# Three load groups, a table of dataless matmuls and new turn strings in a two-layer kernel on one core

## What is computed

```python
mod = (_silu(c) @ wmod).reshape(16, 6, 1, -1)        # per layer: shift, scale and gate, twice
h = _layernorm(x) * (1 + ca) + sa
x = x + ga * attn(h)                                 # ga: sign kept, magnitude at least 0.25
h = _layernorm(x) * (1 + cb) + sb
x = x + gb * ffn(h)
```

## Time and profile before

| | us |
|---|---|
| median of 3 runs | 2970.29 (2969.28 to 2974.66) |
| the profiled execution's own time | 2970.33 |
| its span, first to last instruction | 2968.5 |
| loop of 15 rounds, from 201.9 to 2840.9 | 2639.0 |
| mean granted TensorE clock, share of full | 0.907 |

### The profile page before, as it was taken

One profiled execution on the slowest core, in us unless ns is written; L12 is line 12 of the kernel. 1 busy time (PEld: TensorE's weight loads), 2 busy tenths in 40 slices (PEclk: granted clock), 3 DMA queues, 4 the chain that ended last, 5 costly groups with the idle time before them and its releaser, 6 DMA issues.

```text
span 2968.5 us, 60546 instructions
## 1 busy us (share of the span) xinstructions
PE 2431.9 (82%) x22424; PEld 1916.4 (65%) x22424; DVE 2207.0 (74%) x5056; ACT 1202.5 (41%) x2697; POOL 650.6 (22%) x465
## 2 busy tenths in 40 slices
PE   1478878979887897978889887887988789798897
PEld 1166766757666585756757676675866667576685
DVE  1668777787977778787787877778697777878752
ACT  0333532435344253533525353343534425353432
POOL 0222122131212212122132212213121221312110
PEclk9569989989899998989989998998989899898999
DMA  4000000000000000000000000000000000000000
GB/s 125 2 2 3 1 7 3 7 3 7 2 3 7 3 7 3 1 8 2 8 3 7 2 3 7 3 7 3 7 2 3 7 3 7 3 3 5 1 6 2
DMA packets 24830, 21.39 MB, mean 7 GB/s; under 512 B 7217, under 2 KB 21570, under 8 KB 24530
## 3 DMA queue, kind: packets, MB, share of 16 engines
q1 hardware_dynamic: 24530, 17.26, 2.1%
HBM read 15.13 MB, written 2.13 MB: 6 GB/s over the span
## 4 chain that ended last, share of the span: by engine, by line
PE 42%; issue 27%; DVE 23%; POOL 5%; ACT 2%; SPq 1%; DMA 1%; DVEq 0%; POOLq 0%; ACTq 0%
PE banks L978 6%; PE banks L1151 4%; PE banks L1004 4%; PE banks L1141 4%; PE banks L855 4%; DVE wide L1336 3%; PE banks L970 3%; DVE wide L1324 3%; DVE wide L1344 2%; PE banks L996 2%; PE banks L918 2%; PE banks L960 2%; POOL lg L539 2%; DVE inv L1507 2%; PE banks L927 2%
## 5 line engine op out<-in xcount | busy, mean ns | idle before, releaser
L535 POOL TENSOR_TENSOR wide<-wide 128x512 f32<-128x512 f32 x128 | 260.2, 2033 | 861.0 <-DVE wide L1344 543.5
L1456 DVE SCALAR_TENSOR_TENSOR wide<-pad,conv,wide 128x256 f32<-128x256 f32 x864 | 368.6, 494 | 0.0
L637 ACT ACTIVATE wide<-small,a_neg 128x255 f32<-128x255 f32 x512 | 217.7, 496 | 188.0 <-DVE wide L1336 187.9
L1336 DVE TENSOR_TENSOR_SCAN wide<-wide 128x1024 f32<-128x1024 f32 x128 | 291.6, 2278 | 1.9 <-ACT wide L637 0.3
L762 ACT ACTIVATE inv<-banks,up1b 128x256 f32<-128x256 f32 x512 | 212.1, 489 | 126.6 <-PE banks L1141 126.4
L1141 PE MATMUL banks<-inv,up 128*128 128x256 f32 x1024 | 262.3, 387 | 0.0
L1151 PE MATMUL banks<-down,inv 128*128 128x128 f32 x2048 | 258.9, 277 | 0.0
L1151 PEld LDWEIGHTS banks<-down,inv 128*128 128x128 f32 x2048 | 248.7, 192 | 5.0
L832 PE MATMUL banks<-bc,sel3b 96*128 96x256 bf16 x512 | 110.4, 323 | 162.5 <-DVE wide L1344 134.3
L978 PE MATMUL banks<-inv 64*64 64x64 f32 x5120 | 200.9, 237 | 48.1 <-DVE inv L1507 44.3
L978 PEld LDWEIGHTS banks<-inv 64*64 64x64 f32 x5120 | 184.8, 151 | 73.7 <-issue 73.6
(11 more groups left out here) (277 smaller groups left out, 4966.3 us busy)
## 6 DMA issues: line engine op xcount, KB each, us to landing
gates_bc<-gate_rows SPq DMA_DIRECT2D x32, 128.0 KB, 2.9
up<-in_W SPq DMA_DIRECT2D x1, 2048.0 KB
x<-in_x SPq DMA_DIRECT2D x16, 128.0 KB, 2.2
out<-xn_y SPq DMA_DIRECT2D x16, 128.0 KB, 2.1
wide<-in_wmod SPq DMA_DIRECT2D x2, 384.0 KB
con<-in_con SPq DMA_DIRECT2D x1, 724.0 KB
w_k<-in_Wk SPq DMA_DIRECT2D x1, 512.0 KB
w_q<-in_Wq SPq DMA_DIRECT2D x1, 512.0 KB
```

What stands on the lines that cost most here:

```text
L535: g.tensor_tensor(ypart[p % 2], r[:, 0:512], r[:, 512:1024], ALU.add).then_inc(a_yp.h, 1)
L637: last = s.activation(decay[st % 2][:, at + 1:at + T], dt[:, c, 1:T], ACT.Exp, scale=a_neg[:, c, st * SG + q:st * SG + q + 1])
L1336: v.tensor_tensor_scan(state[st % 2], decay[st % 2], drive[st % 2], 0.0, ALU.mult, ALU.add).then_inc(a_h.h, 1)
L1456: v.scalar_tensor_tensor(dst, src, w, dst, ALU.mult, ALU.add).then_inc(c_conv.h, 1)
```

## The change

- The loads stand in three groups with semaphores of their own: `loaded` (c, `con`, `wmod`), `loaded_first` (12 loads for the first steps) and `loaded_late` (the rest, the two of 2 MB each last). Item 0 is loaded behind the two c's, ahead of the rest. PE waits for `loaded_first` ahead of its first step, and for `loaded_late` ahead of `a_out` of item 0; DVE for the latter ahead of `a_res`, ACT ahead of `c_proj`, each for item 0 only.
- POOL clears its tiles before it waits for `loaded`. DVE's modulation and gate operations move behind `norm2` of item 0 (`a_norm2`); ACT waits for `prep_dve` 8 (scales) in place of 12 (gates).
- `keep_warm` takes its count from a table `WARM` by step, 0 where there is no entry. 33 entries, 55 matmuls per round in place of 40: 27 in the inversion (`lev_Z`, `lev_TT`), 3 ahead of `c_top` of chunk 0, 5 at `a_out`, `b_turn`, `b_logits`, `c_turn` of the first half; none any more at `c_top` of chunk 1, `c_S`, `d_turn`, `d_qkv`, `d_turn_p`, `d_gates`, `d_turn_g`, `d_yinit`.
- The turn strings of PE, DVE and ACT are new; POOL's is the same.

```diff
-FILL = 2
     "tensor": (
-        "yyyyyyyyyyyyxxyyyyyyxyyxyyyyyyxxxyxxyyxxyyyyxxyyxxyyxxyyxxxyxxxxyxyxxyyxxxxyxxyxyxyyyyyxyyxxyyyx"
-        "yyxyyyyxyyxyxyyxyyxyyxyyyxyxyyxyyxxyyyyyxx"),
+        "yyyyyyyyyyyyxxyyyyxyxyyyyyyxyyyxyxyxyxyxxyyyxxyyxxyyxxyxyxxxyxxxyxyxxyyxxxxyxyxyxxyyyxyyxyyxxyyy"
+        "xyyyxyyyyxyyxyyxyyxyyxyyyxyxyyxyyxyxyyyyxx"),
     "vector": (
-        "xyyyyyyyyxyyyyxyyyxyxyyxyyxyyyyxyxyxxyxxyxyxyyxxyxyxxxyyxxxyxxxxxyxxyxyxxyxyxyxxxyxxxyyyxxyxyyxy"
-        "xxxxxyxxyyxxyxxxxxyyyyy"),
+        "xyyyyyyxyyyyyyxyxyxyyxyyxyyyxyyxyxyyxxyyxxyyyxyxxyxyxxxxyyxxxxxyxxxyxxyxyxxyxyxyxxyxxyxxyyxxxyyyxy"
+        "xxxyxxxxyxxyxyxyxxxyyyy"),
+WARM = {
+    ("a_out",): 1, ("b_turn",): 2, ("b_logits",): 1, ("c_turn",): 1, ("lev_Z", 0, 0): 1, ("lev_Z", 0, 1): 3,
+    ("lev_TT", 0, 0): 1, ("lev_TT", 1, 0): 2, ("lev_TT", 1, 1): 1, ("lev_Z", 2, 0): 1, ("lev_Z", 2, 1): 1,
+    ("lev_TT", 2, 1): 1, ("lev_Z", 3, 0): 1, ("lev_Z", 3, 1): 3, ("lev_TT", 3, 0): 3, ("lev_TT", 3, 1): 2,
+    ("lev_Z", 4, 0): 1, ("lev_Z", 4, 1): 2, ("lev_TT", 4, 0): 3, ("lev_TT", 4, 1): 1, ("c_top", 0): 3,
+    ("c_low", 0): 2, ("c_X", 0): 1, ("c_O", 0): 1, ("c_kS",): 2, ("c_low", 1): 2, ("c_X", 1): 2, ("c_O", 1): 2,
+    ("c_turn_o",): 3, ("c_out",): 1, ("d_scores",): 1, ("d_av",): 1, ("d_a",): 2,
+}
...
-            for dst, src in loads:
+            for dst, src in loads[:2]:
                 sp_.dma_start(dst, src).then_inc(loaded, 16)
+            load_x(0)
+            for dst, src in loads[2:]:
+                sp_.dma_start(dst, src).then_inc(loaded, 16)
+            for dst, src in loads_first:
+                sp_.dma_start(dst, src).then_inc(loaded_first, 16)
+            for dst, src in loads_late:
+                sp_.dma_start(dst, src).then_inc(loaded_late, 16)
             sp_.wait_ge(prep_dve, 12)
             sp_.dma_start(gates_dram, gates[:].rearrange("b n d -> b (n d)")).then_inc(gates_stored, 16)
             sp_.wait_ge(gates_stored, 16)
...
-            t.wait_ge(prep_dve, 12)
-            t.wait_ge(prep_act, 7)
             t.wait_ge(prep_pool, 1)
+            t.wait_ge(loaded_first, LOADED_FIRST)
...
+            def a_norm2(i):
+                norm2(i, 0)
+                if isinstance(i, int):
+                    modulation()
+                    gate_rows()
...
-            def keep_warm(bk):
-
-                for _ in range(FILL):
+            def keep_warm(bk, *step):
+
+                for _ in range(WARM.get(step, 0)):
                     t.matmul(bank(bk), identb[:], hideb[:].unsqueeze(1).broadcast_to([P, HG, P]), start=True, stop=True)
```

More of the change, by code:

```diff
@@ L324, in build @@
         gm = sb("gm", [P, 4])
-        loaded = sem("weights_loaded")
+        loaded = sem("modulation_loaded")
+        loaded_first = sem("first_half_loaded")
+        loaded_late = sem("late_weights_loaded")
         mod_done = sem("modulation_products")
@@ L663, in c_proj @@
                 at = m
+                if m == 0 and isinstance(i, int):
+                    s.wait_ge(loaded_late, LOADED_LATE)
                 if m < 9:
@@ L814, in a_xproj @@
             def a_xproj(i):
+                keep_warm(0, "a_xproj")
                 t.wait_ge(a_u.h, a_u.at(i, 1))
@@ L857, in a_out_ @@
             def a_out_(i):
+                keep_warm(0, "a_out")
+                if isinstance(i, int):
+                    t.wait_ge(loaded_late, LOADED_LATE)
                 t.wait_ge(a_ys.h, a_ys.at(i, 2))
@@ L874, in b_up_ @@
                     M = P if m < 4 else H0
+                    if m == 0:
+                        keep_warm(2, "b_up", 0)
                     if m >= 2:
@@ L966, in c_prod @@
                 if n >= 2:
+                    keep_warm(7, "c_prod", gr, half)
                     t.wait_ge(c_AT.h, c_AT.at(i, n - 1))
@@ L1043, in c_S_ @@
             def c_S_(i):
-                keep_warm(7)
+                keep_warm(7, "c_S")
                 t.wait_ge(c_Uw.h, c_Uw.at(i, 1))
@@ L1072, in d_qkv @@
             def d_qkv(i):
-                keep_warm(3)
+                keep_warm(3, "d_qkv")
                 t.wait_ge(ln_h[3].h, ln_h[3].at(i, 1))
@@ L1089, in d_turn_p @@
             def d_turn_p(i):
[L1090 removed]
+                keep_warm(6, "d_turn_p")
                 t.wait_ge(d_p.h, d_p.at(i, 2))
@@ L1110, in d_gates @@
             def d_gates(i):
-                keep_warm(4)
+                keep_warm(4, "d_gates")
                 t.wait_ge(d_xx.h, d_xx.at(i, 1))
@@ L1196, in _, with modulation @@
-            v.wait_ge(silu_c, 5)
-            v.tensor_tensor(gates[:].rearrange("b n d -> b (n d)"), sgn, mag, ALU.mult).then_inc(prep_dve, 1)
-            v.wait_ge(prep_dve, 11)
-            v.tensor_scalar(gates[:, 0, :], gates[:, 0, :], 0.5, None, ALU.mult).then_inc(prep_dve, 1)
-            v.wait_ge(prep_dve, 12)
-            v.wait_ge(prep_act, 7)
-            v.wait_ge(prep_pool, 1)
+            v.wait_ge(prep_pool, 1)
+            def modulation():
+                v.wait_ge(mod_done, 1)
+                v.tensor_copy(shift_scale[:].rearrange("p n b -> p (n b)"), bank(4, 8 * NB)).then_inc(prep_dve, 1)
+                v.wait_ge(prep_dve, 4)
+                for n in range(4):
+                    v.tensor_scalar(shift_scale[:, 2 * n + 1, :], shift_scale[:, 2 * n + 1, :], 1.0, None, ALU.add).then_inc(prep_dve, 1)
@@ L1355, in a_res @@
             def a_res(i):
+                if isinstance(i, int):
+                    v.wait_ge(loaded_late, LOADED_LATE)
                 v.wait_ge(a_out.h, a_out.at(i, 1))
@@ L1637, in d_res @@
                 residual(i, 3, yacc)
-            follow(v, TURNS["vector"], dict(a_norm=lambda i: norm(i, 0), a_norm2=lambda i: norm2(i, 0), a_conv=a_conv_, a_zgate=a_zgate,
+            follow(v, TURNS["vector"], dict(a_norm=lambda i: norm(i, 0), a_norm2=a_norm2, a_conv=a_conv_, a_zgate=a_zgate,
                            a_silu2=a_silu2, a_split=a_split_, a_soft=a_soft1, a_step=a_step, a_scan=a_scan, a_read=a_read, a_y=a_y_, a_res=a_res,
```

115 lines of the change are left out of this document (66 added, 49 removed).

## The result

The changed kernel takes **2871.12 us** (median of 4, 2867.26 to 2875.09) against 2969.78 beside it: ratio 0.9672, 95% interval 0.9644 to 0.9699. The same file run again with other experiments gave 2874.25, ratio 0.9679 (0.9654 to 0.9705). The forecast was 2880.4, 9 us above.

What follows compares the result with a forecast made beforehand. No engine bounds throughout: DVE in the inversion, PE in other stretches, a serial chain between. 2970.3 - 41.4 (start) - 52.5 (15 rounds at -3.5) + 4 (behind the loop) = 2880.4 us, range 2838 to 2938.

Steps and rivals of the forecast that it cites:

- Start: Ahead of the loop: smaller first load groups let ACT write `hT` and the first convolution start 41.4 us earlier.
- Rival 4: At the start: the small load group is held until the bulk has drained, losing 23.6 of 41.4, 2904 us; chance 0.04.
- Pairs removed: In the loop: dataless matmuls that stood in PE's way with inputs ready are taken out, 2.37 us less a round.
- The 27 in the inversion: In the loop: 27 added dataless matmuls, mostly hidden in PE's idle time, cost 0.8 us a round, ends 0 and 5.8.
- Order: In the loop: the new turn strings use up DVE waits, 2.6 us less a round (1.9 and 0.7), ends 0 and 3.5.
- The sum: Per round of the loop: -1.7 net for pairs, -2.6 for order, +0.8 for the inversion's 27, together -3.5 us.
- `c_top` of chunk 0: In the loop: three dataless matmuls ahead of this step, its input ready, cost 0.65 us more a round.
- Behind the loop: Last item's inversion alone, PE-bound: added dataless matmuls exposed but for a few, 4 us more, 131 in place of 127.6.
- 1 (order gives nothing): Rival for the loop: order gains nothing and a round stays at 175.9 us, total 2933; chance 0.22.
- 2: Rival for the loop: the inversion's dataless matmuls lie on the path, 4.1 us more a round, total 2994; chance 0.05.
- 3 (2815 to 2837): Rival for the loop: order at its upper end, nothing exposed, rounds at the fast clock, 6.4 us a round; chance 0.14.

Runs made afterwards that it cites:

- e8: Changed kernel with dataless matmuls put back: two each at `c_S`, `c_top` of chunk 1, `d_qkv`, `d_turn_p`, `d_yinit`, two instead of one at `c_O` of chunk 0; 2904.7 us.
- e5: Changed kernel without the 27 dataless matmuls of the inversion; 2888.1 us, ratio 0.9724.
- f2: Changed kernel with only the inversion's 27 dataless matmuls in the loop and the old table for the last item's second half; 2866.4 us, ratio 0.964.
- e6: Changed kernel with an empty table, no dataless matmul at all; 2877.2 us, ratio 0.9683.
- after: The changed kernel itself, with new loads, new turn strings and new table; 2871.1 us, ratio 0.9672.
- e1: Changed kernel with the old turn strings and old table put back, leaving the new loads and start; 2928.6 us, ratio 0.9869.
- e2: Changed kernel with the old table of dataless matmuls put back, new loads and new turn strings kept; 2904.8 us, ratio 0.9795.
- e4: Changed kernel with the old table for the second half of the last item only; 2866.1 us, ratio 0.9663.
- e3: Changed kernel with the old turn strings put back, new loads and new table kept; 2996.2 us, ratio 1.0106.
- f1: The changed kernel's same file run once more as yardstick; 2874.25 us, ratio 0.9679.

## Why the prediction came out as it did

The total lies 9 us from the forecast, and that is in part luck. The start was 0.9 us better than forecast and the loop 17.2 better, the part behind it 9.2 worse. Within the loop's sum one term had the wrong sign and the terms did not add up.

**Start: right.** `hT` at 17.04 (forecast 17.4), first convolution 20.80 (20.8), loop start 159.6 (near 160). The first group landed by 9.2 (9), the second by 12.95, a little behind the 11 to 12, with nobody late by it: PE's turn needs `xn` and the modulation products, which end at 16.1 as forecast. Rival 4 (completion held until the bulk has drained) is out: the last load was issued at 28, and the groups had released their readers at 9.2 and 12.95. The Trainium skill (DMA: Bandwidth & Descriptors, Queues, rings and completion order) allows completion out of order; here the groups released their readers in the order in which they were issued. PE's wait ahead of `a_out` of item 0 costs nothing; the step is released by DVE:

```profile
80.70 0.38 PE L1040 MATMUL banks<-hideb,identb 128*128 128x512 bf16 x1
82.59 1.13 PE L897 MATMUL banks<-w_out,small 128*128 128x128 f32 x8 [1.51 <-DVE small L1407]
```

**Pairs removed: right.** 2.37 forecast, 2.07 measured (e8).

**The 27 in the inversion: the wrong sign.** The term was +0.8 with ends 0 and 5.8. Measured by e5, beside the 28 others: -1.7; by f2 against e6, alone: 0.0. The step that failed is "DVE is the bound there, so a faster PE in that stretch buys little". It holds for the later levels, where DVE waits under 0.1 us at either clock. It fails at 16 to 31 us of the round, where the strings have DVE wait for the transpose and the split (1.1 us ahead in after), and at the spreads (0.4). The row that I read could not show this: in the round of the earlier trace rows the four waits of DVE that the trace lists in that stretch (0.73 ahead of 1111.54, 1.97 ahead of 1117.45, 0.73 and 0.22 ahead of 1124.45 and 1125.38) all lie outside its two stretches at half clock, 1105.1 to 1108.5 and 1132.4 to 1142.6. The Trainium skill's rule (TensorE: Matmul & The Clock Gate, Why this matters for your kernels), that idle gaps between bursts lower the clock, was weighed and given no share of the sum. The clock of the stretch went from 0.86 to 0.96 while PE's idle time there fell from 13.4 to 7.2 us, as by the rule. I had costed a dataless matmul only as something that can be in the way, its lower end being nothing, and so had left the gain out of the ends.

**Order: right in size, wrong in its parts.** 2.6 forecast, 2.0 measured on its own (e1 to e2; 2.0 again with the empty table; by the medians 1.5 and 2.4). Of it 1.0 is there at the logits (98.35 for 99.30 after the round's start) and 1.0 comes behind, where I had 1.9 and 0.7. DVE's wait of 2.09 ahead of the attention's output in the earlier trace rows was used up as forecast, to 0.7 in e2. In the table's company the back half is worth 2.8 with the new front, four times the 0.7, and 1.3 with the old one. A sum of parts worked out one by one can't show such company; that the missing pairs make the room in PE's queue is my reading, and no run separates it.

**The sum.** From e1's round: strings -2.0, pairs -2.1, the 27 -1.7, and what is left, +1.0, is the rest of the table (`c_top` of chunk 0 was put at +0.65) and what the parts do to each other; together -4.8, against -3.5.

**Behind the loop: too small by 9 us.** Forecast +4, measured +13.2. The inversion's part was read rightly as PE-bound, and it lost 7.7 (the first `c_top` product at 49.6 after the loop's end for 41.8): the 27 and the 3 at `c_top` are 6.5 at full clock, and I had counted the first ones as hidden. Only the very first was, ahead of PE's wait of 4.83; the three behind it were not and ran at half clock, 0.49 each, the others at full clock:

```profile
2747.37 1.98 PE L1020 MATMUL banks<-inv,mats 64*64 64x64 f32 x32 [4.83 <-DVE inv L1557]
2749.28 1.46 PE L1040 MATMUL banks<-hideb,identb 128*128 128x512 bf16 x3
```

The other 5.5 are the clock behind the inversion, which the sum had not asked about. There the last item's steps wait for each other with no second item beside them. From the first `c_top` product on, half clock is 13.7 us of 85.8 before and 36.1 of 91.3 after. Windows of 40 us, 60 us behind the loop's end in both, first before, then after:

```profile
2900.90:2940.90 40.00, 26.46 (x119) 17.43 (x118) 10.55 (x34) 7.83 (x20) 4.64 (x3) 0.83 0.00 0
```

```profile
2788.90:2828.90 40.00, 25.50 (x154) 18.70 (x153) 9.94 (x28) 4.33 (x11) 4.64 (x3) 0.71 0.00 0
```

The old table brings the 12.7 back (e4: 86.5 us from that product on, 22.1 of them at half clock). So it is the changed table, and e5, without the 27, still has 5.8 of the 13.2. But it is not the pairs as such: e8 has eleven of them back and wins 1.3 behind the loop (35.3 us at half clock). Which of the others hold the clock there is open.

**Rivals.** 1 (order gives nothing) is out by e2. 2 was given 0.05; it did not happen, but only because strings and table came together: with the old strings it does (e3). DVE's 4.4 idle us, which I set against it, are those of the old strings, with which it did happen, so they said nothing on it; the place of each entry in PE's queue did. 3 (2815 to 2837) had part of the right mechanism, rounds at the better clock (half clock 28.6 to 18.1 us a round), and too much of it.

## What to carry to other kernels

In this kernel a dataless matmul cost nothing where it stood ahead of a wait in PE's own queue; behind another step's wait it was work on the path, however idle the engine is on average. So read the queue around each one and not the busy share. In this loop a higher share of full clock was worth something only where DVE waited for PE, so look at those waits stretch by stretch. Try the kernel with none at all before tuning their number: here none was within 6 us of a table of 55 and clearly better than the 40 that it replaced. Give the last item a table of its own, since it has no second item to hide or to need the same ones.

## What the runs showed of the hardware

- **The same dataless matmuls hold the clock in one order and not in the other.** The table is the same in e3 and after, half clock 29.6 and 18.1 us a round, of it 11.3 and 3.5 between 43 and 64 us of the round. Windows of 21 us, 46 to 67 us into one round, over later levels of the inversion, first e3, then after. The clock is 0.67 and 0.92, PE busy 13.27 and 18.39:

```profile
924.00:945.00 21.00, 13.27 (x155) 8.33 (x155) 19.45 (x16) 7.65 (x19) 8.59 (x3) 0.67 0.01 2
```

```profile
715.90:736.90 21.00, 18.39 (x278) 12.42 (x279) 21.00 (x20) 9.66 (x23) 6.05 (x4) 0.92 0.01 2
```

- **Less half clock is not time won by itself.** Without dataless matmuls a round of the new strings has 33.8 us at half clock and takes 172.3; with the old table 27.8 and 174.1; with the 27 alone 25.1 and 172.2. From e5 to after half clock falls by 7.2 us between 43 and 64 us of the round, where DVE is busy throughout, and nothing is won there; it falls by 2.0 between 16 and 31 us, where DVE waits for PE and ACT, and 1.1 is won by the split.
- **Rounds of the same code differ by up to 6.6 us.** In after the first round takes 168.6 us and 11 others 170.4 to 170.9; nearly all of them show half clock near 54.5 and 95.5 us of the round. Three take 172.7 to 175.2, and theirs lies at 43 to 61 and 98 to 99. In f1, the same file, five rounds are of the slower kind, and the mean is 171.7 for 171.3. A mean round is a mixture of the two, and a change that only shifts the mixture looks like a gain of some tenths a round.
